# One order of work changed at the end of the up half: weight-block sums moved to GpSimd, softmax and one input split issued later

## What is computed

```
ys  = cond / sqrt(512)
xf  = ((x * ys) @ W_cond) * rsqrt((ys*ys) @ (W_cond*W_cond) + 1e-8)
top = argmax(softmax(xf @ gate_w.T))                  # one of two experts per token
h_e = relu(mask_e(xf) @ w1[e] + b1[e]) ; out_e = h_e @ w2[e] + b2[e]
out = x + sum_e out_e + relu(xf @ sw1 + sb1) @ sw2 + sb2
```

## Time and profile before

| what | us |
|---|---|
| median of three runs (1436.31 to 1439.16) | 1436.5 |
| the profiled execution's own time | 1436.75 |
| its span, first to last instruction | 1433.9 |
| PE busy | 1416.1 (99%) |
| DVE busy | 841.6 (59%) |
| ACT busy | 504.0 (35%) |
| POOL busy | 337.0 (24%) |
| mean granted TensorE clock | 0.996 of full |

### The profile page before, as it was taken

One profiled execution on the slowest core, in us unless ns is written; L12 is line 12 of the kernel. 1 busy time (PEld: TensorE's weight loads), 2 busy tenths in 40 slices (PEclk: granted clock), 3 DMA queues, 4 the chain that ended last, 5 costly groups with the idle time before them and its releaser, 6 DMA issues.

```text
span 1433.9 us, 17720 instructions
## 1 busy us (share of the span) xinstructions
PE 1416.1 (99%) x6262; PEld 1172.4 (82%) x6262; DVE 841.6 (59%) x1338; ACT 504.0 (35%) x776; POOL 337.0 (24%) x378
## 2 busy tenths in 40 slices
PE   9999999999979999999999999999999999999998
PEld 8888878888858888888888888888888888888886
DVE  7978868767877868786855414233164532424225
ACT  4455544545545444445532211112133211211112
POOL 0016000144114200000141521415134051431533
PEclk9999999999989999999999999999999999999999
DMA  6968475766879989786673210203126131220312
GB/s 214 293 192 248 158 249 182 251 208 233 286 218 294 300 263 288 252 253 226 215 218 124 58 35 10 62 16 60 28 69 169 42 68 21 42 46 5 64 22 33
DMA packets 157702, 215.66 MB, mean 150 GB/s; under 512 B 46560, under 2 KB 68576, under 8 KB 157632
## 3 DMA queue, kind: packets, MB, share of 16 engines
q1 hardware_dynamic: 142752, 186.71, 40.6%
q0 software_dynamic: 14880, 28.07, 9.5%
HBM read 131.19 MB, written 85.75 MB: 151 GB/s over the span
## 4 chain that ended last, share of the span: by engine, by line
PE 74%; DVE 2%; issue 1%; POOL 0%; DMA 0%; ACT 0%; POOLq 0%; DVEq 0%; ACTq 0%
PE bank L2019 24%; PE bank L2043 24%; PE bank L1984 21%; PE bank L1947 5%; PE bank L2039 1%; POOL out L793 0%; DVE vb L1378 0%; DVE hl L1345 0%; DMA hidden_scratch<-vb 0%; DVE xw L1314 0%; DVE vb L1372 0%; DMA out<-res,tab 0%; POOL out L796 0%; ACT w_hi L900 0%; DVE res L1774 0%
## 5 line engine op out<-in xcount | busy, mean ns | idle before, releaser
L776 POOL DMA_INDIRECT rows_e<-xf_scratch,soft x144 | 141.6, 983 | 621.3 <-DVE xe_lo L1625 248.1
L1984 PE MATMUL bank<-hl,w_hi 128*128 128x512 f32 x896 | 277.6, 391 | 8.7 <-DVE hl L1345 8.7
L1748 DVE CAST h_hi<-hf 128x512 fp32r<-128x512 f32 (+1 forms) x128 | 57.3, 447 | 386.3 <-ACT hf L1101 348.7
L1101 ACT ACTIVATE hf<-bank,b 128x512 f32<-128x512 f32 (+1 forms) x128 | 87.4, 683 | 546.3 <-PE bank L2019 475.6
L1947 PE MATMUL bank<-xw,w_hi 128*128 128x512 f32 x896 | 276.6, 390 | 2.7 <-ACT vb L983 2.1
L1984 PEld LDWEIGHTS bank<-hl,w_hi 128*128 128x128 f32 x896 | 168.7, 189 | 45.0 <-DVE hl L1345 9.8
L1947 PEld LDWEIGHTS bank<-xw,w_hi 128*128 128x128 f32 x896 | 167.7, 188 | 39.4 <-issue 2.5
L2019 PE MATMUL bank<-xe_lo,w_hi 128*128 128x512 f32 (+1 forms) x512 | 197.7, 386 | 0.0
L2019 PE MATMUL bank<-xe_hi,w_hi 128*128 128x512 f32 (+1 forms) x512 | 197.6, 386 | 0.0
L2019 PE MATMUL bank<-xe_hi,w_lo 128*128 128x512 f32 (+1 forms) x512 | 196.0, 386 | 0.0
L2043 PE MATMUL bank<-w_lo,h_hi 128*128 128x512 f32 x496 | 193.0, 389 | 0.0
(11 more groups left out here) (231 smaller groups left out, 1718.9 us busy)
## 6 DMA issues: line engine op xcount, KB each, us to landing
hin<-hidden_scratch SPq DMA_DIRECT2D x112, 512.0 KB, 4.7
hidden_scratch<-vb SPq DMA_DIRECT2D x80, 512.0 KB, 4.0
hidden_scratch<-vt SPq DMA_DIRECT2D x32, 512.0 KB, 3.9
stage<-w_pack SPq DMA_DIRECT2D x64, 256.0 KB, 3.0
ring<-x_cols SPq DMA_DIRECT2D x32, 256.0 KB, 4.8
xf_scratch<-xo SPq DMA_DIRECT2D x32, 256.0 KB, 4.5
rows<-xf_scratch SPq DMA_DIRECT2D x16, 512.0 KB, 7.4
aux<-w_pack SPq DMA_DIRECT2D x16, 512.0 KB, 4.9
```

Of the source, the lines that this page charges most:

```text
L776: pool.indirect_dma_start(rows_e[:, c % JN, :], None, xf_dram, bass.IndirectOffsetOnAxis(tab_rows[:, c:c + 1], 0)).then_inc(rows_gathered, ...
L1101: nc.scalar.activation(hf[:, j % 2, 0:width(u)], hidden_bank(j, first and e > 0)[:, 0:width(u)], ACT.Relu, bias=b1[:, 1 + e, j:j + 1]).the ...
L1748: nc.vector.tensor_copy(h_hi[:, buf, 0:filled_n], hf[:, j % 2, 0:filled_n]).then_inc(hh_ready, 4)
L1984: last = nc.tensor.matmul(bank[p][:], w[:, DOWN_W[c], i, part], hl[:, n % HL, h, :], start=(i == 0 and q == 0), stop=(i == PAIRS - 1 and q ...
```

## The change

Five edits, none of which changes what is computed:

1. POOL makes the sums of blocks 8 to 13, which DVE made before. Blocks 8 and 9 stand behind the 32 scatters, ahead of the wait for group 14; 10 and 11 behind that wait, ahead of the ten table reads; 12 and 13 behind the table reads, ahead of the wait for their landing.
2. In the last group, DVE's make_t4 of the group before moves from behind the adds of step 5 to behind the first add of step 3, and the sums of block 15 move ahead of make_t1.
3. ACT casts blocks 14 and 15 (raw_hi) around unit 6, ahead of raw_sums_hi of 12 and 13.
4. The exponentials and choose() of the softmax are issued late in group 4.
5. In the last group of blocks 0 to 2, the split of one input operand (block_lo(s+1, 2)) stands two steps later on DVE.

```diff
--- before.py
+++ after.py
@@ -727,7 +727,9 @@
                 raw, out_n = raw_of(n), sums_of(n)
                 a11, a21, a12, a22 = (raw[:, i, :] for i in range(4))
                 pool.wait_ge(raw_in[n], 2 * DMA)
-                pool.wait_ge(sums_made, 4 * n)
+                pool.wait_ge(sums_made, 4 * SUMMED[n])
+                if n >= PAIRS:
+                    pool.wait_ge(up_mm, PER_GROUP * (GROUPS * (BLOCKS - 1) + n % PAIRS // 2 + 1))
                 nc.gpsimd.tensor_tensor(out_n[:, 1, :], a11, a21, ALU.subtract).then_inc(sums_made, 1)
                 nc.gpsimd.tensor_tensor(a21, a21, a22, ALU.add).then_inc(sums_made, 1)
                 pool.wait_ge(sums_made, 4 * SUMMED[n] + 2)
@@ -746,7 +748,11 @@
                 pool.wait_ge(up_mm, PER_GROUP * SCATTER_GROUP + 2 * c)
                 pool.indirect_dma_start(table_dram, bass.IndirectOffsetOnAxis(pos[:, c:c + 1], 0),
                                         ids[:, c * IDW:(c + 1) * IDW], None).then_inc(ids_out, DMA)
+            for n in (PAIRS, PAIRS + 1):
+                raw_sums(n)
             pool.wait_ge(up_mm, PER_GROUP * TABLE_GROUP)
+            for n in (PAIRS + 2, PAIRS + 3):
+                raw_sums(n)
             pool.wait_ge(ids_out, NT * DMA)
             with nc.allow_non_contiguous_dma(reason="one number per 64-byte row"):
                 for i in range(2):
@@ -758,6 +764,8 @@
                         pool.wait_ge(up_mm, PER_GROUP * TABLE_GROUP + 5 * i + q + 1)
                         pool.dma_start(tab_rows[q * B32:(q + 1) * B32, part],
                                        table_dram.rearrange("(c p) w -> p c w", p=B32)[:, part, 0]).then_inc(tab_dma, DMA)
+            for n in (RAW_LAST - 2, RAW_LAST - 1):
+                raw_sums(n)
             pool.wait_ge(tab_dma, 2 * (1 + QD) * DMA)
 
             pool.tensor_scalar(tab_in[:], tab[:], N - 1, None, ALU.min).then_inc(tab_ready, 1)
@@ -982,9 +990,6 @@
                         n = 2 * g + p + PAIRS * h
                         nc.scalar.activation(dst[:, p, :], up_bank(u, UP_BANK[c])[p][:], f, bias=b1[:, 0, n:n + 1]).then_inc(up_kept, 1)
 
-                if u == CHOOSE_GROUP:
-                    act.wait_ge(soft_in, 3)
-                    nc.scalar.activation(soft[:, 3:5, :], soft[:, 1:3, :], ACT.Exp).then_inc(soft_exp, 1)
                 wait(act, t3_out[u % 2], DMA * (u // 2))
                 take(vb11[u % 2], 0, 0, ACT.Identity)
                 if more:
@@ -1022,13 +1027,18 @@
                 for n in jobs[1:]:
                     if not last:
                         raw_sums_hi(n)
+                if u == CHOOSE_GROUP:
+                    act.wait_ge(soft_in, 3)
+                    nc.scalar.activation(soft[:, 3:5, :], soft[:, 1:3, :], ACT.Exp).then_inc(soft_exp, 1)
                 if u == 0:
                     for i in range(RING):
                         act.wait_ge(xf_out[i], DMA * NT // RING)
                 wait(act, t4_out, DMA * u)
                 take(vb21, 6, 1, ACT.Relu)
                 if last:
+                    raw_hi(RAW_LAST)
                     first_units(6, HL)
+                    raw_hi(RAW_LAST + 1)
                     for n in jobs:
                         raw_sums_hi(n)
 
@@ -1065,8 +1075,6 @@
                     wait(act, v_out[0], QD * DMA * s)
                     nc.scalar.copy(v[:, 0, :, p, :], by_token(down_bank(s, 0)[p])).then_inc(dn_kept, 1)
 
-            raw_hi(RAW_LAST)
-            raw_hi(RAW_LAST + 1)
             for s in range(BLOCKS):
                 for c in range(STEPS):
                     for i in range(PAIRS):
@@ -1395,13 +1403,8 @@
                     block_lo(s + 1, 0)
                     x_sum_of(s + 1, 0)
                     x_sum_of(s + 1, 1)
-                for n in jobs:
-                    if n >= PAIRS:
-                        raw_sums(n)
                 if g == 0:
                     block_lo(s, 5)
-                if u == CHOOSE_GROUP:
-                    choose()
                 if u == RANK_GROUP:
                     count()
                 if more:
@@ -1412,8 +1415,6 @@
                 if u > 0:
                     make_t4(u - 1)
                 add(u, vb11[u % 2], 3, 0, 0)
-                if more:
-                    block_lo(s + 1, 2)
                 add(u, vb11[u % 2], 3, 0, 1)
                 for n in jobs[:1]:
                     raw_lo(n)
@@ -1422,10 +1423,13 @@
                     raw_sums_lo(n)
                 add(u, vb22, 4, 2, 1)
                 if more:
+                    block_lo(s + 1, 2)
                     block_lo(s + 1, 3)
                     x_sum_of(s + 1, 3)
                 add(u, vt1, 5, 4, 0)
                 add(u, vt1, 5, 4, 1)
+                if u == CHOOSE_GROUP:
+                    choose()
                 for n in jobs[1:]:
                     raw_lo(n)
                     raw_sums_lo(n)
@@ -1447,22 +1451,20 @@
                 raw_sums(RAW_LAST)
                 units_lo(0, 2)
                 add(u, vb11[u % 2], 3, 0, 0)
+                make_t4(u - 1)
                 units_lo(2, 4)
                 add(u, vb11[u % 2], 3, 0, 1)
                 units_lo(4, 6)
                 add(u, vb22, 4, 2, 0)
                 add(u, vb22, 4, 2, 1)
-                raw_sums(RAW_LAST - 2)
-                raw_sums(RAW_LAST - 1)
                 raw_lo(RAW_LAST - 2)
                 add(u, vt1, 5, 4, 0)
                 add(u, vt1, 5, 4, 1)
-                make_t4(u - 1)
                 raw_lo(RAW_LAST - 1)
+                raw_sums(RAW_LAST + 1)
                 make_t1(u)
                 raw_lo(RAW_LAST)
                 units_lo(6, HL)
-                raw_sums(RAW_LAST + 1)
                 raw_lo(RAW_LAST + 1)
                 make_t2(u)
                 raw_sums_lo(RAW_LAST - 2)
```

## The result

| | us |
|---|---|
| after, median of 4 runs (1459.3 to 1460.41) | 1460.1 |
| before, median of 4 runs beside them (1435.67 to 1439.16) | 1436.4 |
| ratio, 95% interval | 1.0161 [1.0143, 1.0178] |
| the profiled execution after: own time, span | 1459.94, 1457.1 |

The kernel is 1.6% slower. The forecast was 1460.

A forecast was written before the change was run, and what follows sets the result against it. PE was taken to be bound, with 8.7 us of boundary waits on a DVE chain. Loss 26.0 behind POOL's reads, less 2.1 (softmax) and 0.2 (split), gives +23.7 on 1436.75: 1460 us, range 1446 to 1471.

The forecast's parts named there:

- The bound: Start of the down half: PE waits 8.7 us on a DVE chain to unit 7; the change makes unit 7 26.0 us later.
- Softmax and split, -2.3: Up half: the later softmax removes PE's 2.1 us wait in group 4, the later input split a 0.2 us wait.
- Blocks 8 to 11: POOL's sums ahead of the table reads: 359.0 to 378.5, hidden from PE with 1 us to spare, delaying the reads 9.4 us.
- The reads: POOL's ten table reads: about 8 us apart under load, 4.35 once SP pauses; the tenth at 431.3, issue done at 432.5.
- From R to unit 7, 19.15: Boundary: PE resumes unit 7 19.15 us after POOL starts block 12's sums (R, 432.5 on the old clock), at 451.65.
- make_t4 earlier might wait up to 3 us: Last group on DVE: a wait for vb21's landing could hold PE's step 6 by about 1.5 us, inside the wait for POOL.
- The order edits, 4.6 if the chain were DVE's: Last group: earlier make_t4, block 15 and ACT casts, worth up to about 4.6 us, but nothing inside the wait for POOL.
- Slow reads to the end: Rival on POOL's table reads: something other than SP's load paces them, so they stay slow; 1472 us, chance 0.11.
- Reads freed by an idle DVE, 1446: Rival: a busy DVE holds the table reads, so the last five steps fall to about 1.4 us; about 1446, chance 0.08.
- Faster, 1430: Rival: POOL starts blocks 12 and 13 by about 404, unit 7 comes 4.6 us earlier; about 1430 us, chance 0.05.
- The rule that DVE and GpSimd block each other: Two-input DVE and SBUF-reading GpSimd instructions block each other; up to 1 us on top where they meet around block 13.

## Why the prediction was right

**The bound.** That the boundary decides the time, and in it the chain to unit 7, held in every run of the table. From the start of the down half to unit 7 the loss was forecast at 26.0 us and is 26.4. The waits for raw_lo were put at about 23 us and are 26.5; the sum's own numbers already give 24.9 for the first of them (436.9 - 412.0).

**Softmax and split, -2.3.** The place of the softmax was right, and the split was read off the wrong wait. The 0.2 us wait is still there in the kernel after. What the split gave back are three short stalls, 1.2 us in all, that the list of waits does not show. The up half got 3.7 us shorter, so this term was too small by 1.4.

**Blocks 8 to 11.** Forecast 359.0 to 378.5, less the 2.3; they ran from 355.85 to 375.13, 4.8 us a block. The cover of 1 us in group 13 was enough: PE's waits in the up half are 0.2 us in all. The run with these four alone confirms that they cost nothing there.

**The reads.** The first was forecast at 376.3 on the new clock and started at 375.13. The four steps under load were put at 8.0, 8.0, 8.0 and 7.0 and took 8.92, 8.21, 8.43 and 6.50; the five free ones were put at 4.35 each and took 21.3 together. All nine took 53.3, and the sum had 52.7. The choice that decided between 1460 and 1472 was that the pace falls to 4.35 once SP pauses. The run with 32 more transfers and the one with a busy DVE show both halves of its reason: load holds the reads, DVE does not.

**From R to unit 7, 19.15.** Measured 19.30. By its parts: unit 4 at R + 4.48 (4.4), unit 5 at R + 8.76 (raw_lo(13) at 8.6), unit 6 at R + 13.56 (13.2). R itself was 429.59, against 432.5 - 2.3 = 430.2. That this is so close is in part luck: the first read started 1.2 us earlier than forecast, mostly since the up half was shorter, and the reads took 0.6 longer. The agreement of the end to 0.1 us is luck too; the kernel before alone moved by 1.2 us between the sets of runs.

**make_t4 earlier might wait up to 3 us.** It did not wait here. In the version with units 7 and 8 ahead of t2, t4 of the last group did wait, 1.85 us, also for its buffer to be written out.

**The order edits, 4.6 if the chain were DVE's.** Alone they gave 4.8 us of wait and 5.1 by the medians.

**The rivals.** Slow reads to the end: refuted by the steps of 4.2 us. Reads freed by an idle DVE, 1446: DVE had no busy time from 411.5 to 429 and the reads stayed at 4.2 to 4.4. Faster, 1430: the condition was a start of the sums by about 404. With the sums ahead of the reads they start at 395.22 and end at 403.8, and the kernel takes 1426.5, so the rival's mechanism is real; its tenth read would have to start at 403, and it started at 428.45. The rule that DVE and GpSimd block each other (Trainium skill, SBUF — State Buffer, "Who interferes with whom") was to add up to 1 us around block 13: that block took 4.1 us against the 4.0 of the sum, so nothing came on top. The hold itself is there, as the last section shows, but the 4.0 had it already.

## What to carry to other kernels

A free engine is not a free queue: before giving work to an engine that is 24% busy, find what its queue holds at that moment, transfers' issues above all, and put the urgent work ahead of what nobody waits for. Here the same eight operations cost some 32 us behind ten reads and nothing in front of them. The gains of the other edits only show when the late item is out of the way, so split such a change into its parts before it is dropped. And compare the length of a whole stage, not only the list of waits: three stalls worth 1.2 us did not appear in the list.

## What the runs showed of the hardware

**A small strided read holds POOL's queue, and longer when the DMA engines are loaded.** A read of 2304 numbers of 4 bytes lets the next one start after 4.2 to 4.4 us with nothing else running, after 6.5 to 9 us in the loaded stretch of the kernel after (up to 9.95 before), and once after 25.5 us beside a string of 512 KB copies. The lists of transfers after give its landing, and that of a write of 512 KB, and POOL's timeline of the run with four reads gives three issues in a row of copies within SBUF:

```profile
soft<-token_table POOLq DMA_DIRECT2D x8, 9.0 KB, 3.9
...
hidden_scratch<-vb SPq DMA_DIRECT2D x80, 512.0 KB, 3.9
...
408.89 1.54 POOL L772 DMA_DIRECT2D soft<-soft  x3
```

The 9 KB take as long as 512 KB, so it is not the bytes. The copies are 18 KB each in rows of 576 bytes, and POOL issued the three within 1.54 us. So not every small transfer holds the queue. That the many pieces of the table reads do it is likely, but no run changed the pieces alone, and what limits them was not tried.

**Where float32 operations with two inputs meet on DVE and POOL, the later one is held about as long as the other lasts.** The kernel after shows it in two lines given above. DVE's raw_lo(12) starts at 432.70 and takes 1.23 us, as it does alone. POOL's first sum of block 13 starts at 432.73 and takes 1.78, where such a sum takes 0.73 undisturbed. If it could only begin when DVE was done, it would end at 434.7 (an estimate from these numbers); it ends at 434.5. It goes the other way too. With the sums ahead of the reads, DVE's splits read:

```profile
395.30 2.37 DVE L1351 TENSOR_TENSOR hl<-hin,hl 128x512 fp32r<-128x512 f32 x2
...
414.66 1.89 DVE L1351 TENSOR_TENSOR hl<-hin,hl 128x512 fp32r<-128x512 f32 x3
```

Two splits take 2.37 us at 395.30, and three take 1.89 at 414.66, where POOL has no operation running. POOL's operations beside the first pair take 1.07 to 1.17 us in place of 0.73 to 0.76, and up to 1.61 a little later. PE's timeline shows what reached it:

```profile
400.68 0.73 PE L1947 MATMUL bank<-xw,w_hi 128*128 128x512 f32 x2 [0.35 <-DVE vb L1384]
```

DVE lost about 1.1 us at this pair alone, and PE waited 0.35 us.

**Undisturbed, POOL takes 0.73 us for a 128 x 256 sum and DVE 0.42**, so four blocks can change hands without loss where neither is awaited, as the run with only blocks 8 to 11 on POOL shows.
